# Weight quantisation taken into the attention stage of a two-layer transformer kernel

## The chip, the cores and the metric

The kernel runs on one core of a Trainium2 chip. The metric is the device time of one execution in microseconds. The kernel before took 911.02 us as the median of three runs (906.23 to 914.33).

## The reference

Two layers work on x of shape (16, 256, 256). Layer 0 adds a product with one context matrix for each token, then a feed-forward of 8 experts of which each token uses one. Layer 1 adds cross-attention with 16 heads, and then a feed-forward whose weights and activations are quantised to NVFP4 and back (blocks of 16, a scale in e4m3 for each block, values in e2m1):

```
s_w  = 448 * 6 / max|w|                       # one for each of the three weight matrices
amax = max|block of 16|;  sc8 = e4m3(clip(amax / 6 * s_w, 0, 448));  dq = sc8 / s_w
q    = sign(w) * round_to_{0,.5,1,1.5,2,3,4,6}(clip(|w| / dq, 0, 6));  result q * dq
out  = x + linear(silu(linear(xn, gate_w)) * linear(xn, up_w), down_w)   # each linear quantises input and weight
```

gate_w and up_w are (1024, 256), down_w is (256, 1024). Quantising them depends on nothing but the weights.

## The kernel before, in words

The kernel has a program for each engine: SyncE (`sp`, loads and stores), GpSimd (`pool`), ScalarE (`act`), TensorE (`pe`) and VectorE (`v`). Each is written out by hand, and an engine runs its instructions strictly in that order. Order between engines comes from counting semaphores (`wait_ge(sem, n)`); no planner is involved. `Steps.link` puts a semaphore on an instruction and waits for it at once on the same engine.

The stages follow each other: the context product and the routing (to about 176 us of the profiled execution), the experts (to 376), attention (to about 632), the quantised feed-forward (to the end). A flag computed on the chip picks the branch `narrow == 1` of attention for this input; only that branch runs.

Attention goes through NB = 16 batches of 256 rows, each in two halves q = 0, 1 of 128 rows. The helper `batch` of each engine does the second steps of batch b-1 and the first of batch b. For one batch of the loop the orders are these.

- TensorE (L1134): `probs_in(b-1,1)` (8 transposes, L1100), `project_turn(b-1,0)`, `queries(b+1)`, `project(b-1,0)`, `score(b,1)`, `weigh(b-1,1)`, then `probs_in(b,0)`, `project_turn(b-1,1)`, `rows_in`, `keys_values` (in every second batch), `project(b-1,1)`, `score(b+1,0)`, `weigh(b,0)`.
- VectorE (L1759 to L1773): `divide(b-1,0)` once `weigh` is done, `shift(b,0)`, `keys_in`, `add_rows(b-1,0)`, `masked(b,1)`, `new_stats(b-1,0)`, `divide(b-1,1)`, `shift(b,1)`, `add_rows(b-1,1)`, `masked(b+1,0)`, `new_stats(b-1,1)`. `add_rows` waits for the projection, adds the bias bo into `fo` (L1730) and `fo` to the rows `X2` (L1732). `masked` (L1709) waits for the scores, and `probs_in(b,0)` waits for `masked(b,1)` and for `exps(b,0)`.
- ScalarE (L711): `probs_out(b-1,1)`, `values_out(b-1,0)`, `queries_out`, `rows_norm`, `exps(b,0)`, `context_out`, `values_out(b-1,1)`, `probs_out(b,0)`, `rows_out`, `keys_out`, `exps(b,1)`.
- GpSimd (L536): in every second batch a copy of context (L534); otherwise it is idle in attention.

The weights are loaded by SyncE at L435 (the last is issued at 388.95 us of the execution). VectorE takes their maxima in batch 15 (`weight_sizes`, L1690, called at L1782), GpSimd reduces them over the partitions (L554). Behind attention, when all engines are through (`s_cdone`), VectorE computes the block scales (`scales`, L1846) and quantises gate and up (`values`, L1876, called at L1928); TensorE turns them (L1251) and ScalarE copies them to `gT`, `uT` (L801). The first block sizes of the activations (`rows_sizes(0)`, L2045, in `halves`, L1939) come after that on VectorE. Down is quantised between the first products (L2051), turned at L1295 and copied at L838.

## Time and profile before

| | |
|---|---|
| runs, us | 906.23, 911.02, 914.33 (median 911.02) |
| profiled execution, us | 915.28, with a span of 913.5 from its first to its last instruction |
| mean granted TensorE clock | 0.856 of full speed |
| busy, share of the span | TensorE 71%, VectorE 73%, ScalarE 45%, GpSimd 14% |
| attention loop, two batches | 25.1 us |
| longest chain, by engine | TensorE 34%, VectorE 25%, issue 16%, ScalarE 7%, DMA 6% |

The profile is of one execution. A granted clock of 1.00 is 2.4 GHz and 0.50 is 1.2 GHz, TensorE's two levels; other values are means over a stretch in which it changed. In rows of the timeline the first number is the start in us, the second the time from there to the end of the group. Ends of matmuls are modelled. Share of busy time is an average over stages with different limits, so each stage is read by itself.

### The profile page before, as it was taken

Reading aid. Unit: us, or ns where it says so; the run is one execution under the profiler, and the core shown is the slowest. Engines: PE = TensorE matmul, PEld = TensorE weight load, DVE = VectorE, ACT = ScalarE, POOL = GpSimd, SP = SyncE. Lnnn points to the kernel's source line nnn. Section 1 sums busy time; section 2 is a strip of 40 time slices with the busy share of each in tenths; the row PEclk is TensorE's granted clock in tenths of the full one; section 3 lists DMA queues with packets and bytes.
Section 4 is the critical chain, followed back from the end, with each engine's and each line's share of the span. In section 5 each row is a group of like instructions: output and inputs, shape, how many; then the busy total and the mean of one; then the engine's idle time right before and its main releaser. Section 6 shows DMA issues by size and latency. Waiting matters only on the chain.

```text
span 913.5 us, 14032 instructions
## 1 busy us (share of the span) xinstructions
PE 648.0 (71%) x3951; PEld 468.0 (51%) x3952; DVE 663.8 (73%) x1593; ACT 406.8 (45%) x690; POOL 127.7 (14%) x160
## 2 busy tenths in 40 slices
PE   4595867198889998447999999963053565756574
PEld 2383655066566565326888888852021333433243
DVE  5384758555555555474888898895979899999895
ACT  1342321123232232215656666633055779676773
POOL 4534544211212212200000000000000000000000
PEclk9797979599999999867999999995556788877887
DMA  9583443302111111440000000000000000000001
GB/s 323 166 321 120 152 150 117 114 24 57 58 43 52 52 59 58 148 175 1 1 0 0 0 0 0 1 1 3 0 1 0 0 24 23 11 11 23 23 23 47
DMA packets 31511, 54.40 MB, mean 60 GB/s; under 512 B 5022, under 2 KB 24367, under 8 KB 30321
## 3 DMA queue, kind: packets, MB, share of 16 engines
q1 hardware_dynamic: 25328, 39.81, 13.0%
q0 software_dynamic: 5568, 13.58, 4.3%
q10 hardware_dynamic: 576, 0.55, 0.2%
q8 instruction: 18, 0.29, 0.1%
q14 instruction: 21, 0.16, 0.1%
HBM read 39.90 MB, written 15.89 MB: 61 GB/s over the span
## 4 chain that ended last, share of the span: by engine, by line
PE 34%; DVE 25%; issue 16%; ACT 7%; DMA 6%; SPq 4%; another core or an unknown queue 3%; POOL 2%; DVEq 2%; ACTq 0%; POOLq 0%
PE bank L1116 7%; PE quad L947 4%; PE bank L1131 3%; PE quad L1100 3%; PE bank L1074 3%; DVE hh L2006 3%; DMA x_after_ffn<-row,niU 3%; DMA row<-rows_by_expert 2%; PE quad L1091 2%; SPq L415 2%; DVE ctxs L1957 2%; PE bank L1315 2%; POOL x_after_ffn L513 2%; PE quad L1276 1%
## 5 line engine op out<-in xcount | busy, mean ns | idle before, releaser
L1018 PE MATMUL bank<-W2s,hidT 128*128 x320 | 75.9, 385 | 12.2 <-ACT hidT L631 12.2
L1315 PE MATMUL bank<-dT,hqT 128*128 128x256 bf16 x256 | 53.0, 377 | 44.5 <-ACT hqT L845 44.4
L627 ACT ACTIVATE hid<-hid 128x512 f32<-128x512 f32 x40 | 25.3, 632 | 124.3 <-DVE hid L1609 118.2
L1018 PEld LDWEIGHTS bank<-W2s,hidT 128*128 128x128 f32 x320 | 59.1, 190 | 28.4 <-issue 21.7
L1001 PE MATMUL quad<-W1s,xts 128*128 x160 | 72.6, 597 | 0.0
L1116 PE MATMUL bank<-nVB,nPT 128*128 128x34 f32 x512 | 64.6, 282 | 0.0
L1116 PEld LDWEIGHTS bank<-nVB,nPT 128*128 128x128 f32 x512 | 61.4, 196 | 4.0 <-ACT nPT L693 0.2
L513 POOL DMA_INDIRECT x_after_ffn<-row,niU x40 | 39.3, 983 | 168.7 <-DVE row L1618 156.8
L1315 PEld LDWEIGHTS bank<-dT,hqT 128*128 128x128 bf16 x256 | 31.9, 132 | 56.9 <-ACT hqT L845 47.3
L693 ACT COPY nPT<-quad 128x1024 f32<-128x1024 f32 x32 | 32.5, 1015 | 39.5 <-PE quad L1100 39.5
L2006 DVE SCALAR_TENSOR_TENSOR hh<-quad,gmx,sil 128x512 f32<-128x512 f32 x64 | 45.1, 745 | 6.5 <-PE quad L1285 4.9
L1609 DVE TENSOR_TENSOR hid<-quad,b1s 128x512 f32<-128x512 f32 x40 | 27.6, 690 | 30.5 <-PE quad L1001 29.5
L1100 PE MATMUL quad<-ident,nS 128*128 128x128 f32 x256 | 35.3, 282 | 19.2 <-ACT nS L688 19.1
L947 PE MATMUL quad<-ctxs,hid 128*128 x160 | 44.6, 438 | 5.7 <-ACT hid L576 4.7
L947 PE MATMUL quad<-ctxs,xts 128*128 x144 | 41.4, 430 | 6.8 <-issue 5.4
L1001 PEld LDWEIGHTS quad<-W1s,xts 128*128 128x128 f32 x160 | 30.6, 192 | 30.3 <-issue 29.2
L1709 DVE TENSOR_TENSOR nS<-quad,maskS 128x1024 f32<-128x1024 f32 x32 | 38.9, 1217 | 9.7 <-PE quad L1091 9.7
L494 POOL DMA_INDIRECT rows_by_expert<-row,pi x38 | 37.8, 995 | 51.7 <-DVE pi L1502 41.9
L1615 DVE TENSOR_TENSOR oT<-bank,b2s 128x256 f32<-128x256 f32 x40 | 17.0, 425 | 35.8 <-PE bank L1018 27.0
L1718 DVE TENSOR_TENSOR nS<-nS,nM 128x512 f32<-128x512 f32 x64 | 41.4, 688 | 1.1
L817 ACT ACTIVATE sil<-quad,gmx 128x512 f32<-128x512 f32 x64 | 40.5, 683 | 3.8 <-PE quad L1276 2.0
L1285 PE MATMUL quad<-uT,xqT 128*128 128x512 bf16 x128 | 37.3, 397 | 6.7 <-DVE hh L2006 5.4
(326 smaller groups left out, 1485.6 us busy)
## 6 DMA issues: line engine op xcount, KB each, us to landing
row<-rows_by_expert SPq DMA_DIRECT2D x44, 134.0 KB, 2.1
W1s<-in_ctxO SPq DMA_DIRECT2D x4, 1024.0 KB, 7.9
ctxs<-in_ctxT SPq DMA_DIRECT2D x4, 1024.0 KB
W1s<-in_W SPq DMA_DIRECT2D x8, 512.0 KB
W2s<-in_W SPq DMA_DIRECT2D x8, 512.0 KB
X<-x_after_ffn SPq DMA_DIRECT2D x8, 512.0 KB, 8.9
out<-yo SPq DMA_DIRECT2D x16, 256.0 KB, 2.1
b1s<-in_b SPq DMA_DIRECT2D x1, 2048.0 KB
```

The source lines that it names most:

```text
L494: pool.indirect_dma_start(rows_d, bass.IndirectOffsetOnAxis(ap=pi[:, g % 3, u:u + 1], axis=0), row[g % 3][:, u, :], None, bounds_check=E2 ...
L513: pool.indirect_dma_start(x2_d, bass.IndirectOffsetOnAxis(ap=niU[:, h, u:u + 1], axis=0), row[h][:, u, 0:D], None, bounds_check=NT - 1, oo ...
L817: act.activation(sil[:, u % 2, k * 512:(k + 1) * 512], bank[2 + k][:], ACT.Silu, scale=gmx[:, 8:9]).then_inc(s_sil, 1)
L947: ins = pe.matmul(quad[:, u, 0:CW], xz[g % 2][:, u, z, c, :], ctxs[:, bass.ds(ex, 1), c, :].rearrange("p o s -> p (o s)"), start=z + c == ...
L1001: ins = pe.matmul(bank[2 + u % 2][:], xt[h][:, u, c, :], W1s[:, bass.ds(ex, 1), c, :].rearrange("p o s -> p (o s)"), start=c == 0, stop=c ...
L1018: ins = pe.matmul(bank[6 + u % 2][:, 0:D], hidT[:, u % 2, c, :], W2s[:, bass.ds(ex, 1), c, :].rearrange("p o s -> p (o s)"), start=c == 0, ...
L1100: ins = pe.transpose(turned[:, k, c * P:(c + 1) * P], nS[q][:, 4 * k + 2 * c:4 * k + 2 * c + 2, :].rearrange("p h s -> p (h s)"), ident[:])
L1116: ins = pe.matmul(bank[7][:, n * 2 * VW:(n + 1) * 2 * VW], nPT[q][:, k, c * P:(c + 1) * P], nVB[h][:, n, :], start=True, stop=True)
L1315: ins = pe.matmul(bank[(1, 7)[u // 2]][:, (u % 2) * D:(u % 2 + 1) * D], hqT[:, u % 2, c, :], dT[:, c, :], start=c == 0, stop=c == FT - 1)
L1709: tt(nS[q][:].rearrange("p (k m) s -> p k m s", k=4), scored.rearrange("p k (m s) -> p k m s", m=4), maskS[:, q, S - KW:S].unsqueeze(1).un ...
L1718: tt(half, half, bc(nM[q][:, HG * k:HG * k + HG], KW), ALU.subtract).then_inc(n_sub, 1)
L2006: v.scalar_tensor_tensor(hh[u // 2][:, o:o + 512], bank[4 + k][:], gmx[:, 11:12], sil[:, u % 2, k * 512:(k + 1) * 512], ALU.mult, ALU.mult ...
```

## The change

The quantisation of the weights moves into attention, shared by three engines.

- `wraw` is read in PARTS = 4 parts for the block maxima, by VectorE behind the second `shift` of batches 1 to 4 (`weight_sizes(k)`). The maxima of the matrices come from the block maxima (`weight_maxima`) ahead of batch 5, and GpSimd's all-reduce stands at the same place of its program. The scales are computed in batch 5 (`weight_scales`) and 6 (`weight_inverses` between the two halves, `activation_scales` behind the second `shift`).
- The values are made in SLOTS = 8 slots of 768 elements a partition. GpSimd multiplies slot k by the inverse scales (`weight_scaled`, two instructions), ScalarE converts it (`weight_half`), VectorE clamps, rounds and multiplies back (`weight_rounded`, four instructions). VectorE rounds slots 0 to 7 in batches 7 to 14; GpSimd and ScalarE make slot 0 ahead of batch 7 and slots 1 to 7 in batches 7 to 13. There is one buffer `wt` and one `wb1`.
- TensorE turns the result in six groups of 8 transposes in batches 15 and 16 (`weights_in`), and ScalarE copies each (`weights_out`).
- `add_rows` is split: VectorE adds bo into `fo[:, q]`, GpSimd adds `fo` to the rows. `new_stats(b-1,0)` moves behind `divide(b-1,1)`.
- Batches 1 to 6 are written out on VectorE instead of looped. The former `scales` and `values` go, with the transposes and copies of the weights in the feed-forward. Three semaphores of the first stage are replaced by counts on `s_pe0`; the waits stay the same ones.

```diff
 # GpSimd
+            def weight_scaled(k, first=False):
+                if not first:
+                    pool.wait_ge(s_wp, k)
...
+                for to, x, m in zip((wt[:, 0:NGU], wt[:, NGU:NGU + NDN]), src, inv):
+                    ins = pool.tensor_tensor(to.rearrange("p (t k b) -> p t k b", t=x.shape[1], k=BLOCK), x,
+                                             m.unsqueeze(2).broadcast_to([P, m.shape[1], BLOCK, m.shape[2]]), ALU.mult)
+                ins.then_inc(s_wm, 1)
+            def weight_first():
+                pool.wait_ge(s_gs, 1)
+                weight_scaled(0, first=True)
+                def add_rows(b, q):
+                    pool.wait_ge(n_fo, b * 2 + (q + 2))
+                    pool.sem_inc(s_idle, 1)
+                    xr = X2[:, bass.ds(b * 2 + (q + 1), 1), :].rearrange("p o d -> p (o d)")
+                    pool.tensor_tensor(xr, fo[:, q], xr, ALU.add).then_inc(n_fin, 1)
-                def batch(b, p=None):
+                def batch(b, p=None, k=None):
+                    add_rows(b - 1, 0)
                     if p is not None:
                         pool.wait_ge(n_kv, p)
                         context(b + 3)
+                    if k is not None:
+                        weight_scaled(k)
+                    add_rows(b - 1, 1)
...
-                with pool.Fori(0, NB // 2 - 2) as i:
+                with pool.Fori(0, 2) as i:
                     batch(i * 2 + 1, p=i + 2)
+                    batch(i * 2 + 2)
+                weight_maxima()
+                batch(5, p=4)
+                batch(6)
+                weight_first()
+                with pool.Fori(0, SLOTS // 2 - 1) as i:
+                    batch(i * 2 + 7, p=i + 5, k=i * 2 + 1)
+                    batch(i * 2 + 8, k=i * 2 + 2)
+                batch(NB - 3, k=SLOTS - 1)
+                for b in range(NB - 2, NB + 1):
+                    batch(b)
 # ScalarE
+            def weight_half(k, first=False):
+                act.wait_ge(s_wm, k + 1)
+                if not first:
+                    act.wait_ge(s_wq, k)
+                act.mul(wb1[:], top(wt[:]), ABOVE).then_inc(s_wp, 1)
...
+                    if last:
+                        weights_out(0)
+                    if end:
+                        weights_out(3)
                     if not last and not end:
                         queries_out(b + 1, 1 - h)
                         if b is not NB - 2:
                             rows_norm(b + 2)
+                    if k is not None:
+                        weight_half(k)
                     if not end:
                         exps(b, 0)
                     if not last and not end:
                         context_out(b + 1, 1 - h, first=first)
+                    if last:
+                        weights_out(1)
                     if not first:
                         values_out(b - 1, 1)
                     if not end:
                         probs_out(b, 0)
+                    if last:
+                        weights_out(2)
+                    if end:
+                        weights_out(4)
+                        weights_out(5)
...
+                weight_half(0, first=True)
+                with act.Fori(0, 3) as i:
+                    batch(i * 2 + 7, 1, k=i * 2 + 1)
+                    batch(i * 2 + 8, 0, p=i + 5, k=i * 2 + 2)
-                batch(NB - 3, 1)
+                batch(NB - 3, 1, k=SLOTS - 1)
 # TensorE
+            def weights_in(r):
+                if r == 0:
+                    pe.wait_ge(s_wq, SLOTS)
+                if r >= 2:
+                    pe.wait_ge(s_wTe, r - 1)
+                for m in range(8):
...
+                    ins = pe.transpose(bank[(1, 6)[r % 2]][:].bitcast(BF16)[:, o:o + P], wq[:, d:d + P], identb[:])
+                ins.then_inc(s_wT, 1)
 # in batch: groups 0 behind project(14,0), 1 behind weigh(14,1), 2 behind project(14,1),
 # 3 behind project_turn(15,0), 4 behind weigh(15,1), 5 ahead of project(15,1)
...
 # VectorE
+            def weight_scales(steps):
+                v.wait_ge(s_war, 1)
+                steps.link(v.reciprocal(gmx[:, 3:6], gmx[:, 3:6]))
+                steps.link(ts(gmx[:, 3:6], gmx[:, 3:6], FP8_MAX * FP4_MAX, None, ALU.mult))
+                for n in range(3):
+                    ins = ts(tmp[:, spans[n]], amax[:, spans[n]], 1.0 / FP4_MAX, gmx[:, 3 + n:4 + n], ALU.mult, ALU.mult)
+                steps.link(ins)
+                steps.link(ts(amax, tmp, FP8_MAX, None, ALU.min))
+                steps.link(ts(e8.bitcast(I32), amax.bitcast(I32), 0x7F800000, None, ALU.bitwise_and))
+                steps.link(ts(m8_, e8, FP8_NORM, 1.5 * 2.0 ** 20, ALU.max, ALU.mult))
+            def weight_inverses(steps):
+                steps.link(tt(tmp, amax, m8_, ALU.add))
+                steps.link(tt(sc8, tmp, m8_, ALU.subtract))
+                steps.link(ts(tmp, sc8, FP8_TINY, None, ALU.max))
+                steps.link(v.reciprocal(inv8, tmp))
+                ts(wblkb[:], sc8, 1.0 / FINE, None, ALU.mult)
+                for n in range(3):
+                    ins = ts(inv8[:, spans[n]], inv8[:, spans[n]], gmx[:, 3 + n:4 + n], FINE, ALU.mult, ALU.mult)
+                steps.link(ins)
...
+            def weight_rounded(k, steps):
+                v.wait_ge(s_wp, k + 1)
+                steps.link(ts(wb1[:], wb1[:], FP4_MAX * FINE, -FP4_MAX * FINE, ALU.min, ALU.max))
+                steps.link(ts(wb1[:].bitcast(I16), wb1[:].bitcast(I16), GRID, GRID, ALU.add, ALU.subtract))
+                for to, src, m in zip(weight_slot(k, wq), weight_part(wb1), weight_blocks(k, wblkb)):
+                    ins = tt(to, src, m, ALU.mult)
+                ins.then_inc(s_wq, 1)
...
-                def add_rows(b, q):
+                def add_rows(b, q, first=False):
                     v.wait_ge(n_wo, b * 2 + (q + 1))
-                    stn.link(tt(fo[:], bank[0][:, D:2 * D], boS[:], ALU.add))
-                    xr = X2[:, bass.ds(b * 2 + (q + 1), 1), :].rearrange("p o d -> p (o d)")
-                    tt(xr, fo[:], xr, ALU.add).then_inc(n_fin, 1)
+                    if not first:
+                        v.wait_ge(n_fin, b * 2 + (q - 1))
+                    tt(fo[:, q], bank[0][:, D:2 * D], boS[:], ALU.add).then_inc(n_fo, 1)
...
+                def batch(b, h, p, first=False, between=None, behind=None):
+                    divide(b - 1, 0)
+                    shift(b, 0)
+                    keys_in(p, b + 1, 1 - h)
+                    if between:
+                        between()
+                    add_rows(b - 1, 0, first)
+                    masked(b, 1)
+                    divide(b - 1, 1)
+                    new_stats(b - 1, 0)
+                    shift(b, 1)
+                    if behind:
+                        behind()
+                    add_rows(b - 1, 1, first)
+                    masked(b + 1, 0)
+                    new_stats(b - 1, 1)
+                batch(1, 1, 1, first=True, behind=lambda: weight_sizes(0, stn))
...
+                batch(5, 1, 3, behind=lambda: weight_scales(stn))
+                batch(6, 0, 3, between=lambda: weight_inverses(stn), behind=lambda: activation_scales(stn))
+                with v.Fori(0, SLOTS // 2) as i:
+                    stn.enter(i, 2 * (2 + 2 + 2))
+                    batch(i * 2 + 7, 1, i + 4, between=lambda: weight_rounded(i * 2, stn))
+                    batch(i * 2 + 8, 0, i + 4, between=lambda: weight_rounded(i * 2 + 1, stn))
```

## Rows read from the trace of the kernel before

**Rows 1.** Chain of waits, attention loop: start us, us, what.
```profile
443.88 0.91 PE quad L1100 x8
450.75 0.91 PE quad L1100 x8
457.14 0.91 PE quad L1100 x8
462.54 1.00 PE quad L1100 x8
```

**Rows 2.** Busy time by stretch, batch 3: busy us (count), clock, DMA share, GB/s.
```profile
450.00:462.00 12.00, 11.98 (x108) 10.25 (x107) 11.04 (x20) 7.48 (x15) 0.00 (x0) 1.00 0.00 0
```

**Rows 3.** Timeline, end of attention and behind it: start us, us, engine, line, operation.
```profile
609.16 6.66 DVE L1694 TENSOR_REDUCE gmx<-wraw 128x1 f32<-128x2048 f32 x3
...
635.56 10.92 DVE L1857 TENSOR_REDUCE blk<-wraw 128x128 f32<-128x2048 f32 x3
...
646.51 0.68 DVE L1861 TENSOR_SCALAR blk<-blk,gmx 128x128 f32<-128x128 f32 x3
...
648.41 0.56 DVE L1867 TENSOR_TENSOR blk<-blk 128x384 f32<-128x384 f32 x1
...
653.55 2.29 DVE L1900 TENSOR_TENSOR hh<-wraw,blk 128x2048 f32<-128x2048 f32 x1
...
667.20 1.01 DVE L1945 TENSOR_TENSOR ctxs<-ctxs 128x512 bf16<-128x512 bf16 x3 [0.35 <-DVE gmx L1934]
...
637.38 1.06 ACT L793 ACTIVATE ctxs<-x 128x1024 bf16<-128x1024 bf16 x1
```

**Rows 4.** Timeline of VectorE, first half of batch 3.
```profile
453.87 0.42 DVE L1703 TENSOR_TENSOR nKB<-nK,own 128x256 f32<-128x256 f32 x1
...
454.62 0.42 DVE L1730 TENSOR_TENSOR fo<-bank,boS 128x256 f32<-128x256 f32 x1 [0.33 <-PE bank L1131]
...
455.19 0.42 DVE L1732 TENSOR_TENSOR X<-fo,X 128x256 f32 x1
...
455.53 1.22 DVE L1709 TENSOR_TENSOR nS<-quad,maskS 128x1024 f32<-128x1024 f32 x1
```

**Rows 5.** Instructions of GpSimd's drain behind the all-reduce: duration ns min/median/max.
```profile
L555 POOLq DRAIN  x1: 7117/7117/7117, 615.9 to 615.9; - x1
```

**Rows 6.** Timeline of VectorE, first activations.
```profile
672.89 0.43 DVE L1988 TENSOR_SCALAR ctxs<-ctxs 128x1024 int16<-128x1024 int16 x1
673.35 0.69 DVE L1994 TENSOR_TENSOR xq<-ctxs 128x1024 bf16<-128x1024 f16 x1
```

**Rows 7.** Timeline of GpSimd, attention.
```profile
376.91 0.30 POOL L521 MEMSET X<- 128x256 f32 x1
377.16 0.95 POOL L522 MEMSET X<- 128x1024 f32 x1
...
447.53 0.40 POOL L534 COPY nCB<-ctxs 128x256 f32 x1 [23.83 <-PE bank L1066]
```

**Rows 8.** Instructions of L797, duration ns min/median/max, first and last start.
```profile
L797 ACT ACTIVATE ctxs<-x x8: 1056/1056/1057, 671.3 to 866.3; 128x1024 f16<-128x1024 bf16 x8
```

**Rows 9.** Timeline of ScalarE, batch 3.
```profile
455.47 1.14 ACT L688 ACTIVATE nS<-nS 128x512 f32<-128x512 f32 x2
```

**Rows 10.** Timeline: batch 15 starts; last bias addition of attention; first transposes of activations.
```profile
599.91 1.06 PE L1100 MATMUL quad<-ident,nS 128*128 128x128 f32 x8
...
628.30 0.42 DVE L1730 TENSOR_TENSOR fo<-bank,boS 128x256 f32<-128x256 f32 x1 [3.31 <-PE bank L1131]
...
674.16 0.78 PEld L1267 LDWEIGHTS bank<-identb,xq 128*128 128x128 bf16 x8 [6.48 <-issue]
```

**Rows 11.** Busy time by stretch, around two pauses of TensorE.
```profile
612.00:614.00 2.00, 0.00 (x0) 0.00 (x0) 2.00 (x2) 0.72 (x1) 0.00 (x0) 0.77 0.00 0
616.00:624.00 8.00, 5.78 (x22) 5.03 (x22) 2.87 (x8) 0.37 (x1) 0.35 (x1) 0.50 0.00 0
...
418.00:422.00 4.00, 4.00 (x20) 4.00 (x20) 0.00 (x0) 1.80 (x4) 0.00 (x0) 0.51 0.00 0
```

More of the change, by code:

```diff
@@ L551, in _ @@
                 pool.wait_ge(s_cv, NB + 1)
-            pool.wait_ge(s_wmx, 1)
-            pool.partition_all_reduce(gmx[:, 3:6], gmx[:, 0:3], P, bass.bass_isa.ReduceOp.max).then_inc(s_war, 1)
+                weight_maxima()
+                weight_first()
+                for k in range(1, SLOTS):
+                    weight_scaled(k)
             pool.drain().then_inc(s_cdone, 1)
@@ L709, in context_out, with batch @@
                     ins.then_inc(n_va, 1)
-                def batch(b, h, first=False, second=False, p=None, last=False, end=False):
+                def batch(b, h, first=False, k=None, p=None, last=False, end=False):
                     if not first:
@@ L777, in _ @@
                 act.wait_ge(s_fin, 2 * NB)
+                for k in range(SLOTS):
+                    weight_half(k, first=k == 0)
+                for t in range(6):
+                    weights_out(t)
             act.drain().then_inc(s_cdone, 1)
@@ L1145, in batch @@
                         weigh(b - 1, 1 - h, 1)
+                    if last:
+                        weights_in(1)
+                    if end:
+                        weights_in(4)
                     if not end:
@@ L1757, in _ @@
                 masked(1, 0)
[L1758 to L1773 removed]
+                v.wait_ge(n_fo, 1)
+                v.wait_ge(s_wl, 16 * 5)
+                def batch(b, h, p, first=False, between=None, behind=None):
[15 more added lines that the diff above has]
+                batch(1, 1, 1, first=True, behind=lambda: weight_sizes(0, stn))
+                batch(2, 0, 1, behind=lambda: weight_sizes(1, stn))
+                batch(3, 1, 2, behind=lambda: weight_sizes(2, stn))
+                batch(4, 0, 2, behind=lambda: weight_sizes(3, stn))
+                stn.need()
+                weight_maxima()
+                batch(5, 1, 3, behind=lambda: weight_scales(stn))
[4 more added lines that the diff above has]
+                    batch(i * 2 + 8, 0, i + 4, between=lambda: weight_rounded(i * 2 + 1, stn))
+                    stn.leave(SLOTS // 2)
                 b = NB - 1
@@ L2048, in _ @@
             rows_quantised(0)
-            v.wait_ge(s_wT, 2)
-            values((hq[0][:], weights[2][0], wraw[:, 0, :], *weights[2][1:3], 2 * NQ // BLOCK, None, s_wq),
-                   fill=lambda u: product(u, u))
-            v.wait_ge(s_wT, 6)
+            for u in range(4):
+                product(u, u)
             group(0, False)
```

241 lines of the change are left out of this document (99 added, 142 removed).

## The prediction

> **What bounds the kernel now.** I read the chain of waits over the attention loop first. Nearly all its pieces there are TensorE's, back to back. The transposes of L1100 (`probs_in`) mark the half batches: one half lasts 457.14 - 450.75 = 6.39 us, the other 5.40 us in a batch without key projections (3) and 450.75 - 443.88 = 6.87 us in one with them (2) [rows 1]. TensorE is busy 11.98 of 12.00 us there at granted clock 1.00, VectorE 11.04 [rows 2]. So whatever makes TensorE wait in this loop adds to the time, and VectorE work taken away here brings nothing by itself.
>
> The second thing to see is behind attention. After its last statistics VectorE quantises the weights alone: block maxima from 635.56, scales from 646.51, gate and up until the first activation sizes at 667.20. ScalarE had those inputs ready at 637.38 + 1.06 = 638.44 [rows 3]. Ahead of that, the reductions at 609.16 (6.66 us) stand before the last `divide`s [rows 3].
>
> **What it removes.** (a) From 638.5 to 667.20 everything on VectorE is weight work: 28.7 us, all on the path. Down's quantisation, later, goes too, but between the products, which wait for TensorE and ScalarE; I cost it at nothing, and ScalarE's silu order is its cover. (b) The 6.66 us at 609.16. In their place batches 15 and 16 get six groups of 8 transposes, each at most 0.8 us (eight of L1267 took 0.78 in weight loads [rows 10]), and six ScalarE copies of about 1 us. In program order from `probs_in(14,1)` at 599.91 [rows 10]: groups 0 and 1 and the usual half, `probs_in(15,0)` at 607.8; turn, ScalarE's copy and projection of (14,1), group 2, and `weigh(15,0)` ends at 613.5; `exps(15,1)` ends at 613.9 behind copy 2, `probs_in` at 615.0, ScalarE's two copies 616.4, projection 617.5, `weigh(15,1)` 619.4, divide, turn and copy with group 5 beside them 621.5, projection 622.5. So the last `fo` comes at about 622.6 instead of 628.30 [rows 10], 5.7 earlier, all of it at full clock (if that is lost here too, two to three of the 5.7 are). The row addition behind it is GpSimd's now and with its hand-overs 0.5 longer. Net 5.2 us. Removed together: **33.9 us**.
>
> **What it adds, batches 1 to 6.** In the first half of batch 3 VectorE starts `divide` when weigh ends (450.75), comes through `shift` to `keys_in` at 453.87, waits 0.33 us, adds bo at 454.62, rows at 455.19, the mask at 455.53 until 456.75 [rows 4], and `probs_in` follows at 457.14. There is 0.4 us to spare, and 0.6 more since the row addition leaves.
> - *Maxima, batches 1 to 4*, behind the second `shift`. The three reductions at 635.56 cost 10.92 us, so a quarter is 2.73. Without keys: divide 0.7, statistics 0.3 (now ahead), shift 2.5, sizes 2.7, `fo` 0.4, mask 1.2, hand-overs 0.1 = 7.9 against 5.4: 2.5 to 2.6 late. With keys 7.9 against 6.87: 1.05. Twice each: 7.3 us.
> - *Batch 5*: three small reductions ahead of `divide`, where `probs_in` covers only part: 0.7. The all-reduce held GpSimd 7.1 us [rows 5]; the row addition behind it ends 8 us into the batch, and `new_stats(4,0)` waits for it from 7: 1.0. The scales, 648.41 - 646.51 plus 0.4 = 2.3 us [rows 3], behind a shift without keys: 2.1. Sum 3.8.
> - *Batch 6*: the inverses, 653.55 - 648.41 = 5.1 us [rows 3], stand between keys and `fo` of the first half: 5.1 less 1.0 to spare, 4.0. The activation scales (1.0 us) stand where VectorE waits for the projection: nothing.
>
> Together 15.1 us.
>
> **What it adds, batches 7 to 14.** The slots make a new chain, because in batch b ScalarE runs `weight_half(k)` *ahead of* `exps(b,0)`, on which `probs_in(b,0)` waits. `weight_half(k)` waits for GpSimd's `weight_scaled(k)`; this stands behind GpSimd's `add_rows(b-1,0)`; this waits for `n_fo` of the same batch; and VectorE gives that only after `weight_rounded(k-1)`. So four engines that now work side by side work in a row. With the times of batch 3, weigh's end at 450.75 as zero:
> - keys end, VectorE free: 3.5 [rows 4].
> - `weight_rounded`, 768 elements: two scalar operations under the 0.43 us of 1024, and two products that share the 0.69 us of 1024 [rows 6]: 1.4. `fo` ends at 5.3.
> - hand-over 0.2; GpSimd adds 256, then multiplies 512 and 256. No row has an operation of two inputs there. A copy of 256 takes 0.40 [rows 7]; memsets of 256 and 1024 take 0.30 and 0.95 [rows 7], so 0.85 ns an element and stream and 0.18 fixed for the copy. Lowest: one stream, 0.40 + 0.61 + 0.40 = 1.4. Highest: two reads and a write each apart, 0.83 + 1.49 + 0.83 = 3.1. I take the two reads, nearest to the copy with one read: 0.61 + 1.05 + 0.61 = 2.3. GpSimd ends at 7.8.
> - ScalarE's conversion: 1024 cost 1.06 [rows 8], 512 about 0.6 [rows 9]; 768: 0.84. `exps` 1.14 [rows 9]. With hand-overs `probs_in` starts at 9.95 instead of 6.39: **3.6 us late**, 4.0 in batches 7, 9 and 11, where the context copy (0.40) lies in between. Later halves keep their length.
>
> Seven batches (7 to 13): 4 x 3.6 + 3 x 4.0 = 26.4. Batch 14 has only the rounding: 0.2. `weight_half(0)` ahead of batch 7 delays a copy by 0.9, which the slack of the new chain takes up: 0 to 0.5, taken as 0.
>
> The Trainium skill, GPSIMD Engine Reference, section 3.1, says that a two-input add of 2048 fp32 takes 4497 ns on GpSimd against 2293 ns on VectorE, which speaks against moving such work there; no row here shows it. As an estimate by its ratio the three operations would cost about 3.0 us instead of my 2.3, and the sum would be 5 us higher.
>
> **The clock.** TensorE now stands still for 3.5 to 4 us in each of batches 6 to 13. In the pause that the reductions make, the granted clock fell on the way through 612 to 614 (0.77, TensorE busy 0.00). After the pause ahead of 418, TensorE worked 4.00 of 4.00 us at the half level before it had the full one [rows 11], and 4 us at half speed cost 2. In these batches it would hit the second half, which is TensorE's own. I take it for two gaps in three: 8 x 1.3 = 10.4 us. Bounds: 0 (no fall) to 16 (each).
>
> **Sum.** -33.9 + 15.1 + 26.4 + 0.2 + 10.4 = **+18.2 us**. The profiled execution took 915.28 us with a span of 913.5, 4.3 above the median of 911.02, so it would be 933.5; beside the median 929.
>
> **Rivals.**
> 1. *No fall and a quick GpSimd* (about level). With one-stream prices each slot batch is 0.9 us shorter: 7.8 - 6.2 = +1.6, 913. For it: the pauses are short and surrounded by dense work. Against: GpSimd must read both inputs. With my own price of GpSimd and no fall it is +7.8, 919, still within 1%. Chance 0.20.
> 2. *Faster*: the slot chain doesn't reach TensorE. If only the wait of ScalarE for VectorE's rounding (`s_wq`) is late, 0.8 us a batch, the sum is -33.9 + 15.1 + 5.8 = -13, 898. It decides at `weight_half` in batches 7 to 13: GpSimd would have to finish within about 0.2 us of `fo`. For it: GpSimd is idle through the loop (0.00 in [rows 2]) and 28.7 us are surely gone. Against: the copy alone takes 0.40. I leave 0.15, as it would also follow if several of my waits overlap.
> 3. *The clock stays at the half level through the slot batches.* It was 0.50 all through 616 to 624, behind the pause, while TensorE worked 5.78 of the 8 us [rows 11]. Both halves then last about twice 6.4 and 5.4 to 6.9, some 9 us more a batch: 911 + 8 + 63, about 980. Against: the loop's bursts are longer and denser. Chance 0.05.
>
> Forecast 0.60. **Chances.** A measurement of this kernel tells 1% (9 us). Faster 0.15 (rival 2), same 0.20 (rival 1), slower 0.65 (forecast, rival 3). The likeliest case's own range, from the bounds of GpSimd (-6, +6) and of the clock (-10, +6), is 915 to 941. To leave out no more than 0.2, with rival 1 in and rival 2 out, I give 907 to 943.
>
> **What would show it.** In the changed profile: the stretch from attention's end to the first activation sizes about 28 us shorter; no 6.66 us ahead of the last divides; two batches in slots 7 to 12 in 32 us or more instead of 25.1; in them TensorE idle 3 to 4 us before L1100's transposes, released by ScalarE's `exps`, with ScalarE idle before `weight_half`, released by GpSimd. VectorE's 5.1 us in batch 6 seen as a TensorE pause of 4. Granted clock under 1.00 between about 490 and 620. It is wrong if TensorE stays busy in batches 7 to 13, or if the GpSimd products end before ScalarE comes to them.

## The result: 4% slower, twice the predicted loss

The changed kernel took 948.69 us (median of 943.81, 948.83, 948.56 and 949.44) where the kernel before, run beside it, took 912.67 (906.23 to 915.12). The ratio is 1.0395, with a 95% interval of 1.0328 to 1.0461. The forecast was 929 us with a range of 907 to 943: its sign was right, its size was half of what came (36 us instead of 18), and the result lies above the range.

A chip differs from the next by 2 to 3%, so every kernel below is compared by its ratio to the kernel before on the same chip (893 us in the first group of experiments, 914 in the second, 891 in the third); 0.01 is 9 us. Inside a kernel I compare lengths of halves between profiles. The first half of batch b runs from `probs_in(b-1,1)` to `probs_in(b,0)`, the second from there to `probs_in(b,1)`; in the changed kernel `probs_in` is L1193.

The page after, of the profiled execution (943.81 us): busy time by engine and, below, the granted clock in 40 slices.

```profile
span 942.0 us, 14170 instructions
...
PE 669.1 (71%) x3951; PEld 489.4 (52%) x3952; DVE 636.5 (68%) x1583; ACT 413.1 (44%) x698; POOL 164.6 (17%) x208
...
PEclk9797996799999997678897887888956778778787
```

The same lines of the page of the kernel before:

```profile
PE 648.0 (71%) x3951; PEld 468.0 (51%) x3952; DVE 663.8 (73%) x1593; ACT 406.8 (45%) x690; POOL 127.7 (14%) x160
...
PEclk9797979599999999867999999995556788877887
```

VectorE's busy time fell from 663.8 us to 636.5, and TensorE's rose from 648.0 to 669.1 with the same 3951 matmuls. A slower clock does that: the attention loop lies in slices 18 to 27, counted from 0, and instead of the 1.00 that it had [rows 2] these stand at 7 and 8, one of them at 9.

**The tail** did what was forecast, in sum. Timeline of VectorE in the changed kernel: the last bias addition, the first operation behind attention, the first activation sizes.

```profile
683.13 0.42 DVE L1887 TENSOR_TENSOR fo<-bank,boS 128x256 f32<-128x256 f32 x1 [2.12 <-PE bank L1224]
...
691.12 0.39 DVE L2022 RECIPROCAL rs<-sd 128x37 f32<-128x37 f32 x1 [3.85 <-POOLq L610]
...
695.26 1.01 DVE L2035 TENSOR_TENSOR ctxs<-ctxs 128x512 bf16<-128x512 bf16 x3 [3.23 <-ACT ctxs L881]
```

From the last `fo` to the first sizes it is now 12.1 us; before it was 667.20 - 628.30 = 38.9 [rows 3, 10]. From `probs_in(14,1)` (662.63 here) to the last `fo` it is 20.5, before 28.4 [rows 10]. Together 34.7 us are gone there. The row at 691.12 shows a cost that no term had: VectorE waits 3.85 us for GpSimd's closing drain (L610), which begins behind the last row and lasts 6.91 us; before, it waited 2.32 us at this place.

**Attention** took it all back and as much again. From `probs_in(1,0)` to `probs_in(14,0)` (423.27 to 657.36) it lasts 234.1 us where it lasted 162.5: +71.6. Everything behind `probs_in(14,0)` is 34.5 shorter, which leaves 37.1.

**The start** takes some of this back, which nobody forecast. The timeline of GpSimd has the first operation that the program itself writes out at 8.00 us in the kernel before and at 1.13 in the changed one:

```profile
8.00 0.24 POOL L449 IOTA iota_c<- 128x128 f32 x1 [7.51 <-issue]
...
1.13 0.25 POOL L455 IOTA iota_c<- 128x128 f32 x1 [0.64 <-POOLq L2220]
```

TensorE's first matmul follows at 8.81 and at 3.86. This operation stands at 8.00 and 8.08 in the two kernels whose GpSimd program ends with the all-reduce (the one before, and the last experiment below), and at 0.91 to 1.13 in the eleven profiles of all the others. So the late start looks like what the all-reduce of one execution leaves to the next; that is a reading of this pattern, and no run tests it alone. About 4 of the 5.0 us are still there at attention: on one chip `probs_in(0,1)` comes at 392.19 in the last experiment and at 388.45 and 388.26 in the two versions beside it. With it the parts add up to about 33 us, and the ratio's interval is 30 to 42. (The two profiled executions differ by only 28.5 us: the changed one is 8.6 us ahead at `probs_in(1,0)`, 423.27 against 431.87, more than the start accounts for.)

**Two ways of losing time in attention.** One pair of halves of a slot batch shows both ways in which it is lost. Timeline of TensorE, the transposes of L1193 alone, batches 8 and 9:

```profile
548.76 1.97 PE L1193 MATMUL quad<-ident,nS 128*128 128x128 f32 x8 [3.70 <-ACT nS L755]
...
557.63 1.07 PE L1193 MATMUL quad<-ident,nS 128*128 128x128 f32 x8
...
568.33 1.97 PE L1193 MATMUL quad<-ident,nS 128*128 128x128 f32 x8 [4.13 <-ACT nS L755]
```

And two stretches of the same profile (busy time, clock): the first half of batch 9, then its second.

```profile
557.63:568.33 10.70, 6.57 (x57) 5.62 (x56) 9.54 (x18) 5.11 (x10) 2.77 (x4) 0.93 0.00 0
568.33:575.86 7.53, 7.53 (x50) 6.57 (x51) 1.98 (x3) 3.10 (x7) 0.72 (x1) 0.65 0.00 0
```

The first half has a pause of 4.13 us in it. In the second TensorE is busy for all of its 7.53 us, at a clock of 0.65, on work that took 5.47 before at 1.00; eight transposes that take 1.07 at the full level take 1.97 behind the pause. Who makes the pause is read in the chain of waits of the changed kernel, batch 9:

```profile
561.34 0.28 DVE wb L1847
...
562.73 0.43 DVE fo L1887
...
563.44 0.11 POOL X L572
...
564.46 1.75 POOL wt L546 x2
...
566.32 0.07 ACT wb L714
...
567.07 1.14 ACT nS L755 x2
...
568.33 1.75 PE quad L1193 x7
```

This is the chain that the prediction wrote down: rounding, `fo`, GpSimd's row, its slot, ScalarE's conversion, `exps`, `probs_in`. Each link waits for the one before it. The waits of TensorE at L1193 over the whole changed kernel (us in total, times, longest; one of the nine, 19.1 us, is the start of attention, and one at 0.39 is its end) hold both kinds, the slots' and VectorE's pieces in batches 1 to 6:

```profile
PE quad L1193 <- ACT nS L755: 46.5, 9, 19.1
...
PE quad L1193 <- DVE nS L1865: 17.1, 7, 7.7
```

**Batch 5** holds the longest of VectorE's. In the changed kernel's timeline, GpSimd and then VectorE:

```profile
478.77 0.73 POOL L572 TENSOR_TENSOR X<-fo,X 128x256 f32 x1 [8.08 <-DVE fo L1887]
485.15 0.39 POOL L556 PARTITION_ALL_REDUCE gmx<-gmx  x1 [5.66 <-issue]
494.19 0.71 POOL L572 TENSOR_TENSOR X<-fo,X 128x256 f32<-128x256 f32 x1 [8.65 <-issue]
...
494.93 0.43 DVE L1892 BATCH_NORM_STATS2 st<-X 128x6 f32<-128x256 f32 x1 [5.68 <-POOL X L572]
```

GpSimd waits 5.66 us ahead of the all-reduce for nothing that the profile names. Of the 8.65 behind it 0.9 pass until its `fo` is there (485.98 + 0.42 = 486.40), and the other 7.8 have no such reason either. It is 14.7 us from one row to the next, and VectorE's statistics stand there meanwhile with the next shift behind them.

### The profile page after: what moved, and what is told of

Same layout as the page of the kernel before. It is cut to its first block, busy times and chain, and to the rows that moved or that the text cites. A ratio compares the mean times of both kernels' runs of the same rounds, so it can differ in the third digit from the quotient of the medians.

```text
span 942.0 us, 14170 instructions
## 1 busy us (share of the span) xinstructions
PE 669.1 (71%) x3951; PEld 489.4 (52%) x3952; DVE 636.5 (68%) x1583; ACT 413.1 (44%) x698; POOL 164.6 (17%) x208
## 4 chain that ended last, share of the span: by engine, by line
DVE 27%; PE 24%; issue 20%; ACT 8%; DMA 7%; SPq 6%; POOL 3%; DVEq 2%; POOLq 1%; another core or an unknown queue 1%; ACTq 0%
PE bank L1209 3%; PE quad L1193 3%; DMA x_after_ffn<-row,niU 2%; DVE hh L2096 2%; PE quad L1025 2%; DMA row<-rows_by_expert 2%; PE bank L1224 2%; PE bank L1406 2%; SPq L421 2%; DVE nM L1870 2%; DVE ctxs L2047 2%; PE bank L1167 2%; POOL x_after_ffn L519 2%; DMA ctxs<-in_ctxT 2%; PE quad L1374 1%
## 5 line engine op out<-in xcount | busy, mean ns | idle before, releaser
L1193 PE MATMUL quad<-ident,nS 128*128 128x128 f32 x256 | 44.9, 333 | 63.6 <-ACT nS L755 46.5
L1096 PE MATMUL bank<-W2s,hidT 128*128 x320 | 75.9, 385 | 12.3 <-ACT hidT L686 12.3
L1096 PEld LDWEIGHTS bank<-W2s,hidT 128*128 128x128 f32 x320 | 59.1, 190 | 28.4 <-issue 21.7
L1193 PEld LDWEIGHTS quad<-ident,nS 128*128 128x128 f32 x256 | 37.1, 176 | 65.4 <-issue 24.5
L572 POOL TENSOR_TENSOR X<-fo,X 128x256 f32 (+1 forms) x32 | 23.3, 727 | 264.3 <-DVE fo L1887 255.7
L1887 DVE TENSOR_TENSOR fo<-bank,boS 128x256 f32<-128x256 f32 x32 | 13.5, 421 | 58.0 <-PE bank L1224 58.0
```

Source lines behind the costliest of these rows:

```text
L1096: ins = pe.matmul(bank[6 + u % 2][:, 0:D], hidT[:, u % 2, c, :], W2s[:, bass.ds(ex, 1), c, :].rearrange("p o s -> p (o s)"), start=c == 0, ...
L1193: ins = pe.transpose(turned[:, k, c * P:(c + 1) * P], nS[q][:, 4 * k + 2 * c:4 * k + 2 * c + 2, :].rearrange("p h s -> p (h s)"), ident[:])
```

## Experiments

The theory after reading the two traces: all of the loss lies in pauses of TensorE which the *place* of each piece makes, and in the clock that falls behind them. Rivals: GpSimd's arithmetic is too slow wherever it stands; the second halves are long from contention and not from the clock; the work needs room that attention doesn't have.

| kernel | ratio to before (95%) | `probs_in(1,0)` to `(14,0)`, us | pauses, batches 7 to 13, us |
|---|---|---|---|
| before | 1 | 162.5 | 0 |
| changed, again, with the second group | 1.0376 (1.0321 to 1.0432) | 234.4 | 3.5 to 4.1 |
| ScalarE's half behind `exps(b,1)` | 0.9854 (0.9815 to 0.9893) | 192.0 | at most 0.23 |
| GpSimd's slot ahead of its row | 0.9971 (0.9950 to 0.9992) | 202.6 | 0.65 to 0.73, once 1.99 |
| pause filled, 28 matmuls | 1.0325 (1.0283 to 1.0366) | 234.6 | 0 (filled) |
| pause filled, 14 matmuls | 1.0200 (1.0136 to 1.0265) | 218.0 | 0.3 to 0.95 |
| no all-reduce | 1.0286 (1.0245 to 1.0328) | 227.7 | 3.5 to 4.1 |
| VectorE adds the rows | 1.0014 (0.9976 to 1.0051) | 203.0 | 0.73 to 0.94, in batch 7 4.1 |
| all steps moved | 0.9754 (0.9686 to 0.9823) | 176.7 | at most 0.23, in batch 7 1.39 |
| the same, reload hidden | 0.9609 (0.9587 to 0.9630) | 167.2 | at most 0.23, in batch 7 1.39 |
| the same, first slot behind its row | 0.9622 (0.9597 to 0.9647) | 164.4 | at most 0.23 |
| before, with GpSimd's rows alone | 1.0104 (1.0080 to 1.0128) | 162.4 | 0 |

### ScalarE's half moved alone

```diff
-                    if k is not None:
-                        weight_half(k)
                     if not end:
                         exps(b, 0)
...
                     if not end:
                         exps(b, 1)
+                    if k is not None:
+                        weight_half(k)
```

> One move in the changed kernel: ScalarE runs weight_half(k) at the end of its batch, behind exps(b,1), instead of ahead of exps(b,0). Theory A (ScalarE's order makes the chain VectorE - GpSimd - ScalarE - TensorE, and its pauses bring the clock down): the pauses of 3.7 to 4.2 us in batches 7 to 13 go (28.4 us) and with them the longer second halves (14.6 us), less about 0.2 us a batch for VectorE's rounding; 948.7 - 42 = 907 us, and the granted clock is 1.00 from batch 7 on. Rival B (the rounding on VectorE and its contention with GpSimd is what costs): VectorE's work is unchanged, so the time stays above 935 us.

Measured: 0.9854, so one moved call turns a loss of 4% into a gain of 1.5% (expected: 907 of 913, or 0.994; attention fell by the 42 us that were expected). The first halves of batches 7 to 13 are 6.7 us (10.1 to 10.7 in the changed kernel), the second halves 5.3 and 6.8. GpSimd's operations last as long as ever; ScalarE just asks for them later. The first and the second half of batch 9 (busy time, clock):

```profile
527.85:534.56 6.71, 6.57 (x57) 5.61 (x56) 6.22 (x13) 4.25 (x9) 0.90 (x2) 1.00 0.00 0
534.56:539.86 5.30, 5.27 (x51) 4.53 (x51) 5.18 (x9) 3.98 (x8) 2.59 (x4) 1.00 0.00 0
```

Timeline of ScalarE in this kernel: `exps(b,1)`, then the half, which waits for nothing.

```profile
550.71 1.15 ACT L755 ACTIVATE nS<-nS 128x512 f32<-128x512 f32 x2
551.75 0.84 ACT L714 ACTIVATE wb<-wt 128x768 f16<-128x768 bf16 x1
```

What stays over the kernel before, 192.0 - 162.5 = 29.5 us, is nearly all in batches 1 to 6.

### GpSimd's slot ahead of its row

```diff
+                    if k is not None:
+                        weight_scaled(k)
                     add_rows(b - 1, 0)
...
-                    if k is not None:
-                        weight_scaled(k)
                     add_rows(b - 1, 1)
```

> One move in the changed kernel: GpSimd runs weight_scaled(k) ahead of add_rows(b-1,0), so that it no longer waits for fo of the same batch. ScalarE's order stays. Theory A: weight_half(k) then waits only for VectorE's rounding of the slot before; probs_in(b,0) comes about 0.9 us late instead of 3.7 to 4.2, a pause after which the clock doesn't fall: 948.7 - 22 - 15 = 912 us; if the clock falls all the same, 927. Rival: GpSimd's operations themselves are too long wherever they stand (1.74 us and 0.73 us): no gain over 5 us.

Measured: 0.9971. The same chain is cut at another link, since GpSimd no longer waits for `fo` before it multiplies. What is left of the pause is 0.65 to 0.73 us and once 1.99. Behind four of the seven the second half stayed at 5.3 or 6.8; it was longer behind the pause of 1.99 (6.7 instead of 5.3) and behind two of 0.73 (8.4 and 8.3 instead of 6.8). The halves that start at `probs_in(8,0)` and `probs_in(9,0)`, behind pauses of 0.73 and 0.66:

```profile
523.11:531.47 8.36, 8.36 (x63) 7.75 (x63) 4.75 (x8) 3.86 (x9) 1.66 (x2) 0.80 0.00 0
...
538.69:543.98 5.29, 5.27 (x50) 4.52 (x51) 4.83 (x8) 3.11 (x7) 1.65 (x2) 1.00 0.00 0
```

So short pauses can bring the clock down as well, only less often.

### The pause filled

```diff
+                    if fill:
+                        pe.wait_ge(n_qe, b + 2)
+                        for j in range(fill):
+                            pe.matmul(bank[6][:, 0:P], ident[:], ident[:], start=True, stop=True)
                     if not end:
                         probs_in(b, 0)
```

The products are read by nobody. With 28 of them:

> The changed kernel with 28 matmuls of 128 x 128 fp32 that nobody reads, on TensorE in batches 7 to 13 where it waits ahead of probs_in(b,0) (28 x 0.114 = 3.2 us, inside the pauses of 3.7 to 4.2). Nothing that anyone waits for changes. Theory C (the second halves are 1.9 to 2.3 us longer because TensorE comes out of the pause at half clock): they return to 5.4 and 6.9 us, 948.7 - 14 = 935 us, granted clock near 1.00 in batches 7 to 13. Rival D (they are longer because ScalarE and VectorE are late in them): no change, 948 us, or a little more.

A product took 0.226 us where I had taken 0.114, so 28 take 6.3 us, 2 us more than the pause. The first halves grew to 12.7, but the second ones fell to 5.24 and 6.71. The next two runs are the changed kernel itself and the same with 14 products:

> The changed kernel as it is, on the chip of the experiments, where the kernel before takes 893. Every theory expects the ratio of the first chip, 1.040, so about 928; the halves of the batches as in its profile: first halves of batches 7 to 13 of 10.1 to 10.7, second halves of 7.4 and 9.0 where the clock has fallen, 5.3 and 6.8 where it hasn't.

> The changed kernel with 14 matmuls of 128x128 whose output nobody reads ahead of the transposes of probs_in in batches 7 to 13: 14 x 0.226 = 3.2 us, which lies inside pauses of 3.5 to 4.2 us. Theory (the pause costs twice: itself, and the clock that falls behind it): first halves of 10.1 to 10.7 as they are or some tenths less, second halves at 5.3 and 6.8, in all 13 to 18 us faster than the changed kernel. Rival (second halves are long from contention of the engines that catch up): the second halves stay at 7.4 and 9.0, the time is that of the changed kernel within 2 us.

Measured: the changed kernel at 1.0376, where 1.040 was expected, and 932.46 against its 947.41 us on one chip. The two halves of batch 9 with 14 fillers:

```profile
557.90:568.60 10.70, 9.77 (x84) 8.73 (x84) 9.54 (x18) 5.11 (x10) 2.77 (x4) 1.00 0.00 0
568.60:573.90 5.30, 5.27 (x51) 4.53 (x51) 1.98 (x3) 3.11 (x7) 0.73 (x1) 1.00 0.00 0
```

The first half is as long as in the changed kernel to 0.01 us. VectorE, ScalarE and GpSimd do the same in both halves. Only TensorE has something to do in the pause, and the second half is at clock 1.00 and 5.30 instead of 7.53. The sum of the seven second halves fell from 57.7 to 41.5 us. So the clock and not contention is the second loss: 15 us in the slots. The Trainium skill, TensorE: Matmul & The Clock Gate, "HAM oscillation", describes a loop in which each pause lets the clock drop and the next work starts at the half level; the trace agrees, and the fillers show the cause by taking it away.

### No all-reduce

```diff
-                pool.partition_all_reduce(gmx[:, 3:6], gmx[:, 0:3], P, bass.bass_isa.ReduceOp.max).then_inc(s_war, 1)
+                pool.tensor_copy(gmx[:, 3:6], gmx[:, 0:3]).then_inc(s_war, 1)
```

> The changed kernel without the reduction of the maxima over the partitions: GpSimd copies the three columns instead, so each partition has scales of its own. Theory E (the all-reduce holds GpSimd for 14.7 us from the end of batch 4 with the load of its code, and VectorE's new_stats(4,0) waits 5.7 us for the row addition behind it): batch 5's second half, 13.3 us, returns to about 7.8 (the scales stay), with one fall of the clock less: 948.7 - 5.5 - 1.5 = 942 us. Rival F (the wait is the scales' own, for s_war): the time falls by less than 2 us.

Measured: the second half of batch 5 takes 7.53 us instead of 13.31. That half loses 5.8 us by the all-reduce; the others keep their pauses. In this kernel's timeline GpSimd comes from one row to the next without a hole of its own:

```profile
461.55 0.19 POOL L556 COPY gmx<-gmx 128x3 f32<-128x3 f32 x1 [1.11 <-DVE gmx L1796]
467.53 0.73 POOL L572 TENSOR_TENSOR X<-fo,X 128x256 f32<-128x256 f32 x1 [5.79 <-DVE fo L1887]
```

### VectorE adds the rows

```diff
 # GpSimd
-                    add_rows(b - 1, 0)
...
-                    add_rows(b - 1, 1)
 # VectorE, add_rows
                     tt(fo[:, q], bank[0][:, D:2 * D], boS[:], ALU.add).then_inc(n_fo, 1)
+                    v.wait_ge(n_fo, b * 2 + (q + 2))
+                    xr = X2[:, bass.ds(b * 2 + (q + 1), 1), :].rearrange("p o d -> p (o d)")
+                    tt(xr, fo[:, q], xr, ALU.add).then_inc(n_fin, 1)
```

> The changed kernel with the additions of rows back on VectorE, the rest as it is. Theory (the slot is late for what GpSimd does ahead of weight_scaled, 0.73 and its wait for the rows, and for what ScalarE does ahead of the exps, 0.84 and its wait): the pauses of batches 7 to 13 shrink from 3.5-4.2 to 1.5-2.5, the one of batch 5 from 7.7 to about 2 since VectorE no longer waits for a row of GpSimd's; 15 to 30 us faster than the changed kernel. Rival (GpSimd's arithmetic itself, 0.5 to 1.2 an operation, is what the slot waits for): pauses at least 3, under 10 us faster, and those from batch 5.

Measured: 914.44 against 947.41 for the changed kernel on that chip, 33 us and more than the 15 to 30 expected: the pauses of batches 8 to 13 shrank to 0.73 to 0.94, so the clock was kept in most. It is 0.73 us of work that was moved; what counted is that GpSimd's slot no longer stands behind a wait for `fo`. The rival (GpSimd's arithmetic) falls. Batch 7 is the exception: its first half takes 13.9 us, with a pause of 4.1 ahead of `project(6,0)`, because ScalarE waited 6.65 us for the first slot. Timeline: the last of the activation scales on VectorE, which GpSimd's first slot waits for, and that slot.

```profile
512.71 0.21 DVE L1824 TENSOR_SCALAR gmx<-gmx 128x1 f32<-128x1 f32 x1
...
519.97 2.32 POOL L546 TENSOR_TENSOR wt<-wraw,wblk 128x512 f32<-128x512 f32 x2 [36.72 <-issue]
```

The slot starts 7.05 us after it may (512.71 + 0.21), though GpSimd did nothing meanwhile. It is GpSimd's first addition or multiplication since the all-reduce.

### All steps moved

The two moves above; block sizes, maxima and all-reduce ahead of `masked(1,0)`, where VectorE waits 9.7 us; scales and inverses in seven pieces in batches 2 to 6, each no longer than what its half has to spare; VectorE adds the rows of batch 0 itself.

```diff
-                masked(1, 0)
                 v.wait_ge(n_fo, 1)
                 v.wait_ge(s_wl, 16 * 5)
+                for k in range(PARTS):
+                    weight_sizes(k, stn)
+                stn.need()
+                weight_maxima()
+                masked(1, 0)
...
+                batch(1, 1, 1, first=True)
+                batch(2, 0, 1, between=lambda: piece(0), behind=lambda: piece(1))
+                batch(3, 1, 2, between=lambda: piece(2))
+                batch(4, 0, 2, between=lambda: piece(3), behind=lambda: piece(4))
+                batch(5, 1, 3, between=lambda: piece(5))
+                batch(6, 0, 3, between=lambda: piece(6), behind=lambda: activation_scales(stn))
```

Pieces 0 to 6 hold the same instructions as `weight_scales` and `weight_inverses`, the reciprocal in two.

> A version meant to beat both. ScalarE's half behind the exps, GpSimd's half ahead of its row; block sizes, maxima and the all-reduce in the 9.7 us in which VectorE idles ahead of batch 1's mask; scales and inverses in small pieces over batches 2 to 6. Theory (all that the change lost lies in pauses of TensorE that the place of each piece makes, and the clock behind them): no half later than before by over 0.5, 34 us gone from the tail, so 858 to 866 where before takes 893, a ratio of 0.96 to 0.97. Rival (the work costs something wherever it stands, by ports shared or by engines full): 872 to 882, no better than the version with ScalarE's half moved alone (880).

Measured: 0.9754, a gain, but less than the theory's 0.96 to 0.97. The largest hole that was left is in batch 2, where TensorE paused 5.87 us. Timeline of GpSimd, and of VectorE behind it:

```profile
413.51 0.39 POOL L556 PARTITION_ALL_REDUCE gmx<-gmx  x1 [40.83 <-DVE gmx L1798]
...
439.42 0.71 POOL L572 TENSOR_TENSOR X<-fo,X 128x256 f32<-128x256 f32 x1 [25.17 <-issue]
...
440.17 0.43 DVE L1898 BATCH_NORM_STATS2 st<-X 128x6 f32<-128x256 f32 x1 [6.33 <-POOL X L572]
```

The all-reduce was over long before: VectorE read its result at 430.14. `fo` was there at 431.7, and the addition began 7.7 us later. So it is not the all-reduce that blocks here but the first addition behind it. GpSimd's copy at 413.79, between the two, didn't pay for it.

### The reload hidden, and the first slot

```diff
                 weight_maxima()
+                pool.tensor_tensor(warm[:], epsc[:, 0:1], epsc[:, 0:1], ALU.add)
```

> The version with all steps moved, and one GpSimd addition of 128x1 (its result unread) right behind the all-reduce, while GpSimd has nothing else to do. In that version VectorE waited 6.33 us in batch 2 for GpSimd's first row, which began 7.5 us after the fo it adds was there. Theory (the first addition behind an all-reduce pays some 7.5 us for a reload, whenever it comes): the wait is gone, the half at the start of batch 2 takes 5.4 to 6.9 instead of 12.9, the next 6.4 instead of 8.8, the whole 7 to 10 us faster. Rival (the all-reduce itself ran until then, or the wait has another cause): no change.

Measured: 0.9609, the best of all. Timeline of GpSimd:

```profile
396.93 0.39 POOL L557 PARTITION_ALL_REDUCE gmx<-gmx  x1 [41.63 <-DVE gmx L1800]
404.45 0.18 POOL L588 TENSOR_TENSOR warm<-epsc 128x1 f32<-128x1 f32 x1 [7.14 <-issue]
...
415.29 0.73 POOL L573 TENSOR_TENSOR X<-fo,X 128x256 f32<-128x256 f32 x1 [10.30 <-DVE fo L1891]
```

The small addition takes the 7.14 us on itself and the first row waits only for its `fo`. The second half of batch 2, 12.9 us long, became 6.86 and the one behind it went from 8.77 to 6.42; attention is 9.5 us shorter. At 167.2 us it is within 4.7 of the kernel before, so the rival that attention has no room for this work falls too.

The next version moves one slot of GpSimd's back, in batch 7 alone:

```diff
+                    if k is not None and not late:
+                        weight_scaled(k)
                     add_rows(b - 1, 0)
...
+                    if late:
+                        weight_scaled(k)
                     add_rows(b - 1, 1)
```

> The same with one step more: in batch 7 GpSimd scales its slot behind its row, not ahead, so that it doesn't run beside VectorE's shift of that batch. There the shift took 2.16 instead of 1.29 and the keys 0.94 instead of 0.42 while GpSimd multiplied, and TensorE paused 1.39. Theory (two engines slow each other at the same memory): the two halves around batch 7 fall from 8.1 and 7.8 to 6.7 and 5.3, 3 to 4 us. Rival (VectorE was full there anyway): under 1 us. In all 872 to 878 where before takes 914.

With all steps moved, GpSimd's multiplication and VectorE's shift ran at the same time there and both took 0.87 us longer (2.62 for 1.75, 2.16 for 1.29), and VectorE's keys behind the shift took 0.94 for 0.42. Apart, they had their normal lengths, and the two halves fell from 8.1 and 6.6 to 6.7 and 5.3. Attention became 2.7 us shorter, nearly the 3 to 4 expected, yet the time did not move (0.9622 against 0.9609; expected 0.954 to 0.961). Behind `probs_in(14,0)` this kernel is 2.3 us longer with the same work, and the clock differs there. The stretch of 620 to 660 us of the version with the reload hidden:

```profile
620.00:660.00 40.00, 19.29 (x85) 7.29 (x83) 32.63 (x45) 26.86 (x35) 0.00 (x0) 0.76 0.00 0
```

and of this one:

```profile
620.00:660.00 40.00, 17.70 (x80) 7.24 (x79) 33.27 (x49) 26.14 (x33) 0.00 (x0) 0.71 0.00 0
```

Whether a shift of 3 us always costs clock there or only in this execution, one profile of each can't tell; it stays open.

### Before, with GpSimd's rows alone

```diff
 # before; GpSimd
+                    add_rows(b - 1, 0)
...
+                    add_rows(b - 1, 1)
 # before; VectorE, add_rows
-                    stn.link(tt(fo[:], bank[0][:, D:2 * D], boS[:], ALU.add))
-                    xr = X2[:, bass.ds(b * 2 + (q + 1), 1), :].rearrange("p o d -> p (o d)")
-                    tt(xr, fo[:], xr, ALU.add).then_inc(n_fin, 1)
+                    tt(fo[:, q], bank[0][:, D:2 * D], boS[:], ALU.add).then_inc(n_fo, 1)
```

The run also takes `new_stats(b-1,0)` to its later place, behind `divide(b-1,1)`.

> The kernel before with one part of the change alone: GpSimd adds the rows of attention, with two buffers for fo; all of the weights stay where they were. Theory (what the rows cost in the changed kernel, they cost by standing ahead of GpSimd's multiplications; alone they are 0.73 each on an engine without work): within 2 us of before, halves of 6.4 and 5.5 / 6.9 as before or 0.1 less. Rival (the round trip through GpSimd delays the chain itself): every batch 0.3 to 1 us longer, 5 to 15 in all.

Measured: attention is the same to 0.1 us, so the trip through GpSimd costs the loop nothing. Yet the kernel is 1.0% slower. These 8 us lie in the range of the rival, but not by its mechanism: no batch is longer. They are in the tail. Timeline of GpSimd and VectorE:

```profile
604.41 0.72 POOL L541 TENSOR_TENSOR X<-fo,X 128x256 f32<-128x256 f32 x1 [6.56 <-DVE fo L1744]
610.93 0.39 POOL L566 PARTITION_ALL_REDUCE gmx<-gmx  x1 [5.79 <-issue]
...
617.98 0.39 DVE L1859 RECIPROCAL rs<-sd 128x37 f32<-128x37 f32 x1 [10.02 <-POOLq L567]
```

And VectorE at the same place in the kernel before:

```profile
634.33 0.39 DVE L1842 RECIPROCAL rs<-sd 128x37 f32<-128x37 f32 x1 [2.32 <-DVEq L1837]
```

The all-reduce used to start its preparation while GpSimd was idle; now it begins when the last row is done, 5.79 us before the all-reduce itself. GpSimd's closing drain (L567), for which VectorE waits, ends only behind both, so the wait is 10.02 us instead of 2.32. In the changed kernel, whose all-reduce is long over by then, the wait for this drain is 3.85, so about 6 of the 7.7 us are the all-reduce's. The part that looks free takes the cover off something else.

## Why the prediction was half right

Total predicted +18.2, measured +36 by the medians; by the profiles +71.6 in attention, -34.5 behind it and about -4 from the start, +33. The direction and the chain of waits were right. The step that failed is the price of the clock; a second one, smaller, is the price of the all-reduce. Step by step:

- **Removed, 33.9**: measured 34.5. Right in sum, with some luck in the parts: the stretch from the last `fo` to the first sizes lost 26.8 where 28.7 was taken (1.5 of the difference is VectorE's longer wait for GpSimd's drain), the one ahead of it 7.9 where it was 5.2.
- **The start, nothing**: about -4. It stood in no term.
- **Sizes in batches 1 to 4, 7.3**: 7.6. Right, to the pauses of 2.5 and 1.05.
- **Batch 5, 3.1 in its second half**: 7.8. The term "the all-reduce held GpSimd 7.1" was mis-sized. It came from the drain at the end of GpSimd's program [rows 5], and that isn't the all-reduce's price: in the version without an all-reduce the drain is there too, as the row of this instruction shows. From one row to the next GpSimd was held 14.7.

```profile
L610 POOLq DRAIN  x1: 6907/6907/6907, 658.5 to 658.5; - x1
```

- **Batch 6, inverses, 4.0**: 4.0, though not as the pause of 4 that it was to be. TensorE paused 2.07 us; the rest went into its own work, 8.28 us instead of 6.37 at a clock of 0.82.
- **Slots, 3.6 and 4.0 each, 26.4**: 28.3, with pauses of 3.5 to 4.2. The chain was right link by link. GpSimd's three operations took 2.5 us (0.73, and 1.74 for the two multiplications) where I had taken 2.3. By the ratio that the Trainium skill gives for two inputs on GpSimd and VectorE (GPSIMD Engine Reference, section 3.1) the estimate was 3.0. Here 0.73 against VectorE's 0.42 for 256 is 1.7 times.
- **The clock, 10.4**: 22.7, and this is the step that failed. I took two gaps in three at 2 us each, in the second halves of batches 6 to 13 alone. In fact every one of the seven slot pauses brought it (14.6 us), and so did pauses in batches 1 to 6 (about 8.1, worked out as the length over before less pause and maxima in the first halves of batches 2, 4 and 5 and the second of 6): the first half of batch 2, with no pause in it and 2.5 us of pause ahead of it, took 9.1 us instead of 6.4. To those I had given only their own length, but for the one in batch 6. The upper bound that I stated, 16, was for batches 6 to 13 and too low for the whole.

12.3 us of clock, 4.7 for the all-reduce and 1.9 for the slots are 18.9 of the 19.5 by which attention (71.6) exceeded the forecast (52.1). The first rival (quick GpSimd, no fall) fails on both of its conditions, and the second, that the chain doesn't reach TensorE, by 26.3 us of ScalarE's waits for GpSimd. The third (half speed throughout) was wrong, too: the level came back before each second half was over.

## What to carry to other kernels

When work is slipped into a loop that one engine bounds, write for each piece who waits behind it in the *program order* of every engine it touches; here one call ahead of `exps` instead of behind cost 42 us of attention with the same instructions. Price a pause of TensorE twice, once as it is and once as the clock that falls behind it; in the loops of all these runs every pause of 2 us and more, if nothing filled it, cost TensorE another 0.9 to 2.8 us behind it. Short ones are not safe either: of thirteen pauses between 0.65 and 0.94 us (GpSimd's slot ahead of its row, and VectorE adding the rows) ten cost only themselves, but of the fourteen of about 1.05 us in batches 2 and 4 of seven profiles thirteen were followed by a half at a clock of 0.79 or 0.80. And before giving an idle engine small steps, look for what its idleness covers.

## What the runs showed of the hardware

- GpSimd pays twice around an all-reduce. Ahead of it these are 5.66 us in the changed kernel and 5.79 with the rows alone, unless GpSimd is idle long before. Behind it they fall on the first addition or multiplication, whenever that comes: 7.8 us in the changed kernel, 7.05, 7.7 and 7.14 in three others. Copies between the two did not pay it (413.79 in the version with all steps moved). Each of the two stretches begins with two records MODIFY_POOL_CONFIG of GpSimd's sequencer (in the changed kernel at 479.45 and 479.48, and at 486.63 and 486.67); from the second one it is 5.6 to 5.7 us to the all-reduce and 6.7 to 7.5 to the addition. The Trainium skill, GPSIMD Engine Reference, section 2.1, gives about 6 us for the first call of loaded code, behind such a record. The trace agrees ahead of the all-reduce; that the way back is paid too, and takes longer, is not told of there. That it is a reload of code is my reading of these records; the runs show the time, and that a small addition takes it away.
- GpSimd's drain at the end of its program takes 6.91 us in the changed kernel and in the one without an all-reduce, and 7.12 in the kernel before. What it spends them on is not shown.
- A product of 128x128 in fp32 takes 0.226 us of TensorE and stands in the trace as two records; a transpose of the same shape is one, and at the same clock they start 0.11 us apart.
- VectorE's operations and GpSimd's multiplications slowed each other where they overlapped. In batch 7 with all steps moved GpSimd lost 0.87 us and VectorE 0.87 in the shift and 0.52 in the keys. In both, and at three more places in batch 7 of the version in which VectorE adds the rows (keys 1.28 for 0.42, the int16 step of the rounding 1.21 for 0.36, a row addition 0.95 for 0.42), VectorE's operation ended 0.2 to 0.6 us behind the end of the multiplication that was running when it began. Beside VectorE's reductions both kept their lengths (1.74 and 1.20 us in batch 9 of the changed kernel).
